# A fused conv, attention and FFN kernel: q, k and v kept in SBUF, twelve units of projections ahead, and a rewritten first seven units

## The chip, the cores and the metric

The kernel runs on one core of one Trainium2 chip. The metric is the device time of one launch in microseconds (us); lower is better. Engines: PE is the matrix engine (PEld its weight loads), DVE the vector engine, ACT the scalar engine, POOL the GpSimd engine, SP the engine whose queue issues most DMAs.

## The reference, cut to what matters

The input x is 64 batches of 64 rows by 1024 values, all in 32-bit floats.

```python
# per batch b, in this order
y   = agg_w[b] @ x + agg_b[b]                      # 64x64 mixing of the rows, from a small MLP on cond
q   = einsum('bsD,Ddh->bsdh', y, Wq) + bq          # 32 x 32 heads;  k, v: 32 values a row
p   = softmax(einsum('bsdh,bse->bsde', q, k) / sqrt(32))   # summed over the heads, so q is 32 values a row
x   = x + broadcast(einsum('bsde,bse->bsd', p, v)) # o: 32 values a row, each repeated 32 times
c   = grouped_conv1d(x, 4 groups, 9 taps) + context(b) + bias
out = x + c @ (scale * (unpacked 4-bit weights - zero_point)).T + bias
```

The softmax works on 32 by 32 values for each of the 4096 rows, and the product with the 1024 by 1024 weights on all rows.

## The kernel before

**Tiling.** A unit is four batches, 256 rows, in two tiles of 128 rows (t = 0, 1). There are 16 units (`NU`) and 32 tiles (`k = 2 * unit + t`). What each unit goes through:

- PE, `project`: z = x times the summed q, v, k weights, 32 matmuls in all (two records for each of 16); ACT copies z from PSUM to SBUF (`z_copy`). PE, `mix`: the mixing over rows, into the PSUM bank `p_sm`.
- DVE, attention: `softmax_top` (adds the bias to q, k, v and finds a bound of each row's scores, a chain of small operations), then for each tile `score` (q times k, 1024 values a partition), `subtract` (the bound), ACT's `exp`, and again on DVE `sum_exp`, `times_v`, `sum_v`, `divide`, which gives o.
- o has to be spread over the channel layout of the convolution. SP's queue writes it to DRAM (`save_o`) and reads it back, repeated, as `o_c` (`spread_o`).
- POOL: `add_o` adds `o_c` to `xc` (three operations for each of four channel groups g), ACT makes the high part `c_hi` (`c_high`), POOL the low part `c_lo` (`c_low`). POOL also makes x + bias (`x_bias`) and adds o there (`x_o`) for the residual.
- PE, `conv`: 6 matmuls of 512 columns for each g. ACT `u_copy`, DVE `turn_u` (a transpose into PSUM), ACT `u_high`, DVE `u_low`. PE, `linear(k, slot)`: 8 slots of 4 matmuls, 512 columns each, for a tile. DVE `finish` adds the result to the residual, SP stores it.

**What sets the order.** Every engine runs a list of calls written out by hand. For the first units it is a written list (SP, POOL, ACT, DVE and PE each have theirs); from unit 5 of the attention on, a loop with a fixed order per unit. An engine starts an instruction when the one before it has left and the semaphores it waits for have come.

**Where operands lie.** In the kernel before, q and v of a unit stay in the PSUM bank `p_sm`, as does the bound `top` from unit 2 on (units 0 and 1 have it in SBUF, `top_own`); only k is copied to SBUF (`k_sb`, L812). The sum `num` is in PSUM as well. So DVE's `score` (L828) reads `p_sm` and `k_sb`, `subtract` (L833) `prob` and `p_sm`, `times_v` (L841) `prob` and `p_sm`, `divide` (L860) `p_sm` and `rden`. POOL's operands are all in SBUF. Only units 1 and 0 have some `subtract` calls on POOL (L476).

**The first unit** is special: its o doesn't go over DRAM. PE copies it with a selection matrix (`copy_o`, L1217) and DVE adds it to `xc` out of PSUM (`add_first`, L868, eight operations). Unit 1's tile edges and two `c_low` calls of position p = 2 are DVE's (L876, L882); both operands of these four instructions are in SBUF.

Of the kernel before, what the change touches and what calls it, by code (L numbers as in the profile page):

```python
# [44 lines left out]

def block_program(nc, xt_in, xc_in, cols, mix_w, wq, wvk, conv_w, ctx_w, packed_t, xn_in, bias_in, out):
    ctx = ExitStack()
    with ctx:
# [1417 lines left out]
```

## Time and profile before

| | |
|---|---|
| time, median of 3 runs | 431.02 us (429.46 to 432.3) |
| the profiled execution's own time | 432.14 us |
| its span, first to last instruction | 430.2 us |
| mean granted PE clock | 0.992 |
| busy in the span: PE, DVE, POOL, ACT | 412.6, 363.5, 340.9, 226.8 us |

Busy time of an engine is the time in which at least one of its instructions is in the engine. Matmul records overlap each other, so a PE that is busy all the time is only at its pace if the number of its matmuls in a stretch says so too. The duration of a DVE or POOL instruction includes any time that it stands in its engine and can't go on, which the views of idle time and waits don't show; it shows where the same shape takes longer in one place than in another.

### The profile page before, as it was taken

The page shows a single profiled execution, that of the slowest core. Times are in us where ns is not written, and L with a number is a line of the kernel's source. Part 1 is how long each engine was busy: PE and PEld are TensorE (multiplying, and loading weights), DVE is VectorE, ACT ScalarE, POOL GpSimd, SP SyncE. Part 2 cuts the span into 40 slices and gives each one's busy share as a digit, 9 for nine tenths or more (in the row PEclk, how much of TensorE's full clock was granted, in tenths as well). Part 3 has the DMA queues.
Part 4 walks back from the last instruction along what each step waited for, and adds up shares of the span by engine and source line. Part 5 has one row for each costly group of instructions (what it writes and reads, how often), then busy time and mean ns, then how long its engine had stood idle before and what let it go on. Part 6 is the DMA issues. An engine that isn't in the chain of part 4 may idle for free.

```text
span 430.2 us, 6661 instructions
## 1 busy us (share of the span) xinstructions
PE 412.6 (96%) x2195; PEld 348.8 (81%) x2195; DVE 363.5 (85%) x603; ACT 226.8 (53%) x465; POOL 340.9 (79%) x316
## 2 busy tenths in 40 slices
PE   3969899899999999999999999999999999999997
PEld 2969799778888888888888888888888888888885
DVE  2896999998989899899989799998989799983421
ACT  3854655556455274657446365647264465562700
POOL 4033948769686999999999979899979979999920
PEclk9988999999999999999999999999999999999999
DMA  8989246470637565664736290928174371816112
GB/s 312 385 330 379 102 149 225 146 270 5 182 106 265 192 220 202 181 240 143 281 100 223 62 350 20 329 88 259 63 237 185 69 254 38 287 41 234 48 52 98
DMA packets 21752, 79.05 MB, mean 184 GB/s; under 512 B 5704, under 2 KB 5832, under 8 KB 17352
## 3 DMA queue, kind: packets, MB, share of 16 engines
q1 hardware_dynamic: 21416, 77.21, 51.2%
q10 hardware_dynamic: 288, 1.18, 0.9%
q8 instruction: 33, 0.54, 0.5%
q14 instruction: 15, 0.12, 0.1%
HBM read 61.11 MB, written 17.27 MB: 182 GB/s over the span
## 4 chain that ended last, share of the span: by engine, by line
PE 79%; DVE 6%; DMA 2%; issue 1%; POOL 1%; ACT 0%; DVEq 0%; POOLq 0%
PE p_f L1159 51%; PE p_conv L1153 19%; PE p_sm L1129 7%; PE p_sm L1138 1%; DMA o_c<-o_dram 1%; DMA o_dram<-o_sb 1%; DVE den L837 1%; DVE c_lo L882 1%; DVE xc L876 1%; DVE prob L828 1%; DVE prob L833 1%; DVE p_sm L845 1%; POOL xc L440 0%; DVE p_ut L893 0%; DVE prob L841 0%
## 5 line engine op out<-in xcount | busy, mean ns | idle before, releaser
L1159 PE MATMUL p_f<-w_ffn,u_hi 128*128 128x512 f32 x512 | 195.8, 392 | 0.0
L1159 PE MATMUL p_f<-w_ffn,u_lo 128*128 128x512 f32 x512 | 194.9, 390 | 0.0
L610 ACT ACTIVATE u_sb<-p_conv,u_bias,cols_sb 128x128 f32<-128x128 f32 x256 | 95.0, 460 | 42.2 <-PE p_conv L1153 40.2
L1159 PEld LDWEIGHTS p_f<-w_ffn,u_lo 128*128 128x128 f32 x512 | 96.2, 188 | 20.5
L1159 PEld LDWEIGHTS p_f<-w_ffn,u_hi 128*128 128x128 f32 x512 | 96.1, 188 | 20.5
L453 POOL TENSOR_TENSOR c_lo<-xc,c_hi 128x516 fp32r<-128x516 f32 (+1 forms) x66 | 82.7, 1263 | 11.6 <-ACT c_hi L600 6.8
L464 POOL TENSOR_TENSOR xn<-xn,bias_n 128x1024 f32<-128x1024 f32 x32 | 76.3, 2403 | 4.7 <-DMA xn<-xn_in_in 4.6
L600 ACT ACTIVATE c_hi<-xc 128x516 fp32r<-128x516 f32 (+1 forms) x68 | 41.0, 608 | 65.0 <-POOL xc L445 59.8
L440 POOL TENSOR_TENSOR xc<-xc,o_c 128x384 f32<-128x384 f32 x60 | 54.3, 905 | 24.5 <-DMA o_c<-o_dram 23.3
L906 DVE TENSOR_TENSOR xn<-p_f,xn 128x512 f32<-128x512 f32 x64 | 43.4, 678 | 23.8 <-PE p_f L1159 23.4
L893 DVE STREAM_TRANSPOSE p_ut<-u_sb 128x512 f32<-128x512 f32 (+1 forms) x68 | 45.8, 680 | 16.4 <-ACT u_sb L610 16.3
L471 POOL TENSOR_TENSOR xn<-xn,o_sb 128x1024 f32<-128x1024 f32 x30 | 57.1, 1922 | 0.2
L1153 PE MATMUL p_conv<-c_hi,cw_hi 128*128 128x512 f32 (+1 forms) x136 | 54.2, 399 | 2.0 <-DVE c_lo L882 1.2
L619 ACT ACTIVATE u_hi<-p_ut 128x512 fp32r<-128x512 f32 (+1 forms) x68 | 39.2, 577 | 31.5 <-DVE p_ut L893 31.1
L1153 PE MATMUL p_conv<-c_lo,cw_hi 128*128 128x512 f32 (+1 forms) x136 | 52.4, 385 | 0.0
L1153 PE MATMUL p_conv<-c_hi,cw_lo 128*128 128x512 f32 (+1 forms) x136 | 52.4, 385 | 0.0
L1129 PEld LDWEIGHTS p_sm<-w,xt 128*128 128x128 f32 x416 | 49.6, 194 | 2.5 <-issue 1.5
L1129 PE MATMUL p_sm<-w,xt 128*128 128x96 f32 x416 | 50.0, 277 | 0.9 <-issue 0.8
L592 ACT ACTIVATE prob<-prob 128x1024 f32<-128x1024 f32 x32 | 33.8, 1055 | 24.9 <-DVE prob L833 21.2
L897 DVE TENSOR_TENSOR u_lo<-p_ut,u_hi 128x512 fp32r<-128x512 f32 (+1 forms) x68 | 42.3, 641 | 0.3 <-ACT u_hi L619 0.3
L837 DVE TENSOR_REDUCE den<-prob 128x32 f32<-128x1024 f32 x32 | 37.9, 1208 | 1.4 <-ACT prob L592 1.3
L845 DVE TENSOR_REDUCE p_sm<-prob 128x32 f32<-128x1024 f32 x32 | 38.9, 1216 | 0.1
(113 smaller groups left out, 458.6 us busy)
## 6 DMA issues: line engine op xcount, KB each, us to landing
xc<-xc_in_in SPq DMA_DIRECT2D x16, 1032.0 KB, 8.8
xn<-xn_in_in SPq DMA_DIRECT2D x16, 1024.0 KB, 7.1
out<-xn SPq DMA_DIRECT2D x31, 512.0 KB, 7.0
xt<-xt_in_in SPq DMA_DIRECT2D x15, 1024.0 KB, 5.6
o_c<-o_dram SPq DMA_DIRECT2D x15, 256.0 KB
xn<-wq_in SPq DMA_DIRECT2D x4, 512.0 KB, 12.4
xt<-wq_in SPq DMA_DIRECT2D x1, 1024.0 KB, 6.8
xn<-wq_in SPq DMA_DIRECT2D x1, 1024.0 KB, 8.8
```

The costliest lines, as they stand in the source:

```text
L440: eng.tensor_tensor(x4[:, :, :, 0:3], x4[:, :, :, 0:3], o.unsqueeze(3).broadcast_to([P, UB, DH, 3]), ALU.add).then_inc(s_add, 1)
L453: eng.tensor_tensor(rows_of(c_lo, p, g), rows_of(xc[:, unit_of(p) % 2, :, :, :], p, g), rows_of(c_hi, p, g).bitcast(F32), ALU.subtract).th ...
L464: eng.tensor_tensor(x, x, bias_n[:, :], ALU.add).then_inc(s_xb, 1)
L471: eng.tensor_tensor(runs, runs, o_val(k).unsqueeze(2).broadcast_to([P, DH, D // DH]), ALU.add).then_inc(s_xo, 1)
L610: ins = eng.activation(u_sb[:, g % 2, i * P:(i + 1) * P], p_conv[g % 2][:, i * P:(i + 1) * P], ACT.Identity, bias=u_bias[:, g, bat:bat + 1 ...
L845: eng.tensor_reduce(num(a)[:, t, :], prob[:, t, :, :], AX.X, ALU.add).then_inc(s_num, 1)
L893: eng.transpose(columns(p_ut[g % 2], p), columns(u_sb[:, g % 2, :], p)).then_inc(s_ut, 1)
L897: eng.tensor_tensor(ut_view(u_lo, p, g), columns(p_ut[g % 2], p).rearrange("p (n r c) -> p n r c", n=len(batches(p)), r=R), ut_view(u_hi, ...
L906: eng.tensor_tensor(x, p_f[half][:, :], x, ALU.add).then_inc(s_res, 1)
L1129: last = mm(z_ps(a)[:, t * W3:(t + 1) * W3], xt[:, a % NXT, r, t * P:(t + 1) * P], w3[:, r, :], start=(r == 0), stop=(r == R - 1))
L1153: last = mm(columns(p_conv[g % 2], p), w[:, shift, g, :], rows_of(src, p, g)[:, :, shift:shift + P], start=(n == 0), stop=(n == 5))
L1159: return mm(p_f[half][:, :], u[:, (k // TU) % 2, r, t * P:(t + 1) * P], w_ffn[:, r, 512 * half:512 * half + 512], **flags)
```

## The change

1. **q, k, v, the bound and num in SBUF.** `softmax_top` adds the bias in one operation from PSUM into a new SBUF tile `qkv_sb` (two buffers). `score`, `subtract`, `times_v` and `divide` now read `qkv_sb`, `top_own` and `num`, all in SBUF. The column sums that the bias needs are kept in SBUF too (`col_sb`). One PSUM bank then serves the mixing of all units, and `mix(a)` waits only until unit a - 1's bias is added.
2. **z up to 12 units ahead** (`NZ` 7 to 12), with three x buffers in place of two; units 0 to 10 are projected in the written part.
3. **o of unit 0 over DRAM too** (`spread_first`, one transfer for each tile); `copy_o` and `add_first` are gone, and POOL's `add_o` does positions 0 and 1 as well (8 groups of three half-size operations).
4. **A new beginning**: q weights in nine transfers, sums over heads interleaved with the small MLP, the context weights with the other small inputs, zero-point work on POOL, and warming matmuls before the first real ones.
5. **New written lists** for the first seven units on all engines; the loops start later, with the same order inside.
6. **The last half tile in quarters**: the second half of tile 31 in two pieces of 256 columns, each added and stored by itself.

```diff
-        k_sb = sb("k_sb", [P, TU, DH])
+        num = sb("num", [P, TU, DH])
+        qkv_sb = sb("qkv_sb", [P, 2, TU, W3])
+        col_sb = sb("col_sb", [P, W3])
...
         def qkv(a):
-            return p_sm[a % 2][:, 0:TU * W3].rearrange("p (t w) -> p t w", t=TU)
+            return qkv_sb[:, a % 2, :, :]
...
         def top(a):
-            return p_sm[a % 2][:, TU * W3:TU * W3 + TU * DH].rearrange("p (t d) -> p t d", t=TU)
...
+            return top_own[:, a % 2, :, :]
...
                 for t in range(TU):
-                    eng.scalar_tensor_tensor(out=qkv_bias[:, t, :], in0=col3(a if a else 1), scalar=mix_bias[:, TU * a + t:TU * a + t + 1],
+                    eng.scalar_tensor_tensor(out=qkv_bias[:, t, :], in0=col_sb[:, :], scalar=mix_bias[:, TU * a + t:TU * a + t + 1],
                                              in1=bias3[:, :], op0=ALU.mult, op1=ALU.add).then_inc(s_qb, 1)
...
-                eng.tensor_tensor(k_sb[:, :, :], qkv(a)[:, :, 2 * DH:W3], qkv_bias[:, :, 2 * DH:W3], ALU.add).then_inc(s_qkv, 1)
-                eng.tensor_tensor(qkv(a)[:, :, 0:2 * DH], qkv(a)[:, :, 0:2 * DH], qkv_bias[:, :, 0:2 * DH], ALU.add).then_inc(s_qkv, 1)
+                eng.tensor_tensor(qkv(a), mixed_ps(), qkv_bias[:, :, :], ALU.add).then_inc(s_qkv, 1)
...
-                eng.tensor_tensor(prob[:, t, :, :], down(qkv(a)[:, t, 0:DH]), along(k_sb[:, t, :]), ALU.mult).then_inc(s_score, 1)
+                eng.tensor_tensor(prob[:, t, :, :], down(qkv(a)[:, t, 0:DH]), along(qkv(a)[:, t, 2 * DH:W3]), ALU.mult).then_inc(s_score, 1)
...
-                eng.tensor_reduce(num(a)[:, t, :], prob[:, t, :, :], AX.X, ALU.add).then_inc(s_num, 1)
+                eng.tensor_reduce(num[:, t, :], prob[:, t, :, :], AX.X, ALU.add).then_inc(s_num, 1)
...
-                eng.tensor_tensor(o_val(k), num(a)[:, t, :], rden[:, t, :], ALU.mult).then_inc(s_o, 1)
+                eng.tensor_tensor(o_val(k), num[:, t, :], rden[:, t, :], ALU.mult).then_inc(s_o, 1)
...
-NZ = 7
+NZ = 12
+LAST = ((0, 512), (512, 768), (768, 1024))
...
+            def spread_first(t):
+                eng.wait_ge(s_ow, 16 * (t + 1))
+                eng.dma_start(o_c[:, 0, t * TN:(t + 1) * TN, :, :].rearrange("p n g d -> p (n g d)"),
+                              o_dram[0, :, t * TN * G:(t + 1) * TN * G, :].rearrange("c k d -> c (k d)").unsqueeze(0).broadcast_to([R, CG, TN * G * DH])).then_inc(s_oc_first[t], 16)
```

**DVE in the loop, the second tile's scores to the first o.** The names are those of the list above; `xn<-p_f,xn` is `finish`. Before:

```order
L828 TENSOR_TENSOR prob<-p_sm,k_sb 128x1024
L833 TENSOR_TENSOR prob<-prob,p_sm 128x1024
L906 TENSOR_TENSOR xn<-p_f,xn 128x512
L837 TENSOR_REDUCE den<-prob 128x32 x2
L841 TENSOR_TENSOR prob<-prob,p_sm 128x1024 x2
L845 TENSOR_REDUCE p_sm<-prob 128x32
L906 TENSOR_TENSOR xn<-p_f,xn 128x512
L849 RECIPROCAL rden<-den 128x32
L860 TENSOR_TENSOR o_sb<-p_sm,rden 128x32
```

The same place in the changed kernel:

```order
L960 TENSOR_TENSOR prob<-qkv_sb 128x1024
L965 TENSOR_TENSOR prob<-prob,top_own 128x1024
L1024 TENSOR_TENSOR xn<-p_f,xn 128x512
L969 TENSOR_REDUCE den<-prob 128x32 x2
L973 TENSOR_TENSOR prob<-prob,qkv_sb 128x1024 x2
L977 TENSOR_REDUCE num<-prob 128x32
L1024 TENSOR_TENSOR xn<-p_f,xn 128x512
L981 RECIPROCAL rden<-den 128x32
L987 TENSOR_TENSOR o_sb<-num,rden 128x32
```

The order is the same. In the four kinds of `TENSOR_TENSOR` other than `finish`, the operand that was in PSUM (`p_sm`) is now in SBUF (`qkv_sb`, which `score` reads twice, `top_own`, `num`).

**DVE in the loop, `softmax_top`.** Before:

```order
L802 SCALAR_TENSOR_TENSOR qkv_bias<-p_sm,mix_bias,bias 128x96 x2
L812 TENSOR_TENSOR k_sb<-p_sm,qkv_bias 128x64
L813 TENSOR_TENSOR p_sm<-p_sm,qkv_bias 128x2x64
L817 TENSOR_REDUCE k_max<-k_sb 128x2
L817 TENSOR_REDUCE k_min<-k_sb 128x2
L821 TENSOR_TENSOR p_sm<-p_sm,k_max 128x64
L821 TENSOR_TENSOR top<-p_sm,k_min 128x64
L823 TENSOR_TENSOR p_sm<-p_sm,top 128x64
```

In the changed kernel:

```order
L937 SCALAR_TENSOR_TENSOR qkv_bias<-col_sb,mix_bias,bias 128x96 x2
L945 TENSOR_TENSOR qkv_sb<-p_sm,qkv_bias 128x192
L949 TENSOR_REDUCE k_max<-qkv_sb 128x2
L949 TENSOR_REDUCE k_min<-qkv_sb 128x2
L952 TENSOR_TENSOR top_own<-qkv_sb,k_max 128x64
L952 TENSOR_TENSOR top<-qkv_sb,k_min 128x64
L954 TENSOR_TENSOR top_own<-top_own,top 128x64
```

One operation fewer, and five of the seven two-operand ones now have both tensors in SBUF.

**DVE at the start, from the bound of unit 1 to o of unit 0's second tile.** Before:

```order
L823 TENSOR_TENSOR top_own<-p_sm,top 128x64
L868 TENSOR_TENSOR xc<-p_f,xc 128x2x129
L837 TENSOR_REDUCE den<-prob 128x32
L828 TENSOR_TENSOR prob<-p_sm,k_sb 128x1024
L841 TENSOR_TENSOR prob<-prob,p_sm 128x1024
L868 TENSOR_TENSOR xc<-p_ut,xc 128x2x129
L845 TENSOR_REDUCE p_sm<-prob 128x32
L868 TENSOR_TENSOR xc<-p_ut,xc 128x2x129
L868 TENSOR_TENSOR xc<-p_f,xc 128x2x129
L849 RECIPROCAL rden<-den 128x32
L854 TENSOR_TENSOR o_first<-p_sm,rden 128x128
```

In the changed kernel:

```order
L954 TENSOR_TENSOR top_own<-top_own,top 128x64
L977 TENSOR_REDUCE num<-prob 128x32
L981 RECIPROCAL rden<-den 128x32
L987 TENSOR_TENSOR o_sb<-num,rden 128x32
L969 TENSOR_REDUCE den<-prob 128x32
L960 TENSOR_TENSOR prob<-qkv_sb 128x1024
L973 TENSOR_TENSOR prob<-prob,qkv_sb 128x1024
L977 TENSOR_REDUCE num<-prob 128x32
L981 RECIPROCAL rden<-den 128x32
L987 TENSOR_TENSOR o_sb<-num,rden 128x32
```

`add_first` (L868) is gone from DVE, and the bound of unit 1 comes before the last steps of unit 0's first tile.

## Rows read from the trace of the kernel before

**Rows 1.** The page, part 1: busy us (share of the span) and number of instructions.
```profile
PE 412.6 (96%) x2195; PEld 348.8 (81%) x2195; DVE 363.5 (85%) x603; ACT 226.8 (53%) x465; POOL 340.9 (79%) x316
```

**Rows 2.** Windows: stretch, its length, busy us (instructions), granted clock, DMA share, GB/s.
```profile
0.00:40.00 40.00, 29.49 (x246) 27.69 (x247) 25.40 (x54) 24.04 (x30) 9.83 (x12) 0.91 0.90 356
106.18:380.22 274.04, 274.04 (x1345) 229.41 (x1344) 255.00 (x418) 148.75 (x314) 249.68 (x239) 1.00 0.53 180
```

**Rows 3.** Timeline of DVE and POOL, 66 to 79 us: start, duration, engine, instruction.
```profile
66.04 0.90 POOL L440 TENSOR_TENSOR xc<-xc,o_c 128x384 f32<-128x384 f32 x1 [7.03 <-DMA o_c<-o_dram]
66.15 1.74 DVE L876 TENSOR_TENSOR xc<-xc,o_c 64x512 f32<-64x512 f32 x1
67.01 1.51 POOL L440 TENSOR_TENSOR xc<-xc,o_c 128x384 f32<-128x384 f32 x1
67.92 1.53 DVE L876 TENSOR_TENSOR xc<-xc,o_c 64x512 f32<-64x512 f32 x1
...
70.62 0.69 DVE L882 TENSOR_TENSOR c_lo<-xc,c_hi 128x516 fp32r<-128x516 f32 x1
...
72.14 4.74 POOL L464 TENSOR_TENSOR xn<-xn,bias_n 128x1024 f32<-128x1024 f32 x2
...
74.62 2.82 DVE L882 TENSOR_TENSOR c_lo<-xc,c_hi 128x516 fp32r<-128x516 f32 x1
...
76.82 1.76 POOL L453 TENSOR_TENSOR c_lo<-xc,c_hi 128x516 fp32r<-128x516 f32 x1
```

**Rows 4.** DVE's groups by shape: instruction, count, busy us, mean ns, idle before.
```profile
L828 DVE TENSOR_TENSOR prob<-p_sm,k_sb 128x1024 f32<-128x1024 f32 x32 | 38.6, 1207 | 0.0
L841 DVE TENSOR_TENSOR prob<-prob,p_sm 128x1024 f32<-128x1024 f32 x32 | 37.7, 1210 | 0.0
L833 DVE TENSOR_TENSOR prob<-prob,p_sm 128x1024 f32<-128x1024 f32 x28 | 33.8, 1209 | 0.4
L802 DVE SCALAR_TENSOR_TENSOR qkv_bias<-p_sm,mix_bias,bias 128x96 f32<-128x96 f32 x32 | 8.6, 309 | 6.9 <-PE p_sm L1138 6.0 <-PE p_sm L1252 0.9
L860 DVE TENSOR_TENSOR o_sb<-p_sm,rden 128x32 f32<-128x32 f32 x30 | 5.8, 192 | 2.8
L868 DVE TENSOR_TENSOR xc<-p_f,xc 128x258 f32<-128x258 f32 x4 | 1.7, 415 | 1.0 <-PE p_ut L1217 1.0
L833 DVE TENSOR_TENSOR prob<-prob,top_own 128x1024 f32<-128x1024 f32 x1 | 1.2, 1224 | 0.0
```

**Rows 5.** POOL's groups by shape, with the same columns.
```profile
L464 POOL TENSOR_TENSOR xn<-xn,bias_n 128x1024 f32<-128x1024 f32 x32 | 76.3, 2403 | 4.7 <-DMA xn<-xn_in_in 4.6
L453 POOL TENSOR_TENSOR c_lo<-xc,c_hi 128x516 fp32r<-128x516 f32 x58 | 76.2, 1323 | 4.8 <-POOL xc L445 2.0
L471 POOL TENSOR_TENSOR xn<-xn,o_sb 128x1024 f32<-128x1024 f32 x30 | 57.1, 1922 | 0.2
L440 POOL TENSOR_TENSOR xc<-xc,o_c 128x384 f32<-128x384 f32 x60 | 54.3, 905 | 24.5 <-DMA o_c<-o_dram 23.3
L443 POOL TENSOR_TENSOR xc<-xc,o_c 64x128 f32<-64x128 f32 x56 | 29.4, 525 | 0.0
```

**Rows 6.** Timeline of DVE at the start: the wait for unit 1's mixing, unit 1's last o.
```profile
36.30 0.54 DVE L802 SCALAR_TENSOR_TENSOR qkv_bias<-p_sm,mix_bias,bias 128x96 f32<-128x96 f32 x2 [2.97 <-PE p_sm L1138]
...
57.54 0.19 DVE L860 TENSOR_TENSOR o_sb<-p_sm,rden 128x32 f32<-128x32 f32 x1
```

**Rows 7.** Timeline at the end: the last o, POOL's add and last c_lo, DVE's last u_lo.
```profile
381.88 0.19 DVE L860 TENSOR_TENSOR o_sb<-p_sm,rden 128x32 f32<-128x32 f32 x1
...
389.49 0.89 POOL L440 TENSOR_TENSOR xc<-xc,o_c 128x384 f32<-128x384 f32 x1
...
401.44 1.31 POOL L453 TENSOR_TENSOR c_lo<-xc,c_hi 128x516 fp32r<-128x516 f32 x1
...
409.68 0.68 DVE L897 TENSOR_TENSOR u_lo<-p_ut,u_hi 128x512 fp32r<-128x512 f32 x1
```

**Rows 8.** The chain that ended last, from 406 us on: start us, us, what.
```profile
406.05 20.91 PE p_f L1159 x92
426.95 0.02 issue
426.98 0.69 DVE xn L906
```

More of the change, by code:

```diff
@@ L380, in _ @@
             spread_o(3)
+            store(0)
             load_c(4)
@@ L1006, in _ @@
             u_low(2, 1)
-            score(3, 1)
-            turn_u(2, 3)
             finish(1, 0)
             u_low(2, 2)
+            subtract(3, 1)
+            turn_u(2, 3)
+            sum_exp(3, 0)
             u_low(2, 3)
-            subtract(3, 1)
+            times_v(3, 0)
+            sum_exp(3, 1)
+            sum_v(3, 0)
             finish(1, 1)
-            sum_exp(3, 0)
-            turn_u(3, 0)
-            sum_exp(3, 1)
-            times_v(3, 0)
-            finish(2, 0)
             times_v(3, 1)
-            u_low(3, 0)
@@ L1033, in _ @@
             turn_u(3, 3)
+            sum_exp(4, 0)
             u_low(3, 2)
[L1035 removed]
             u_low(3, 3)
[L1037 removed]
+            sum_exp(4, 1)
+            times_v(4, 0)
             finish(3, 1)
[L1039 to L1046 removed]
+            times_v(4, 1)
+            sum_v(4, 0)
+            divide(4, 0)
@@ L1047, in _ @@
+            sum_v(4, 1)
+            divide(4, 1)
+            finish(4, 0)
             turn_u(4, 0)
-            divide(4, 1)
-            finish(4, 1)
             softmax_top(5)
-            turn_u(4, 1)
             u_low(4, 0)
             score(5, 0)
+            turn_u(4, 1)
+            finish(4, 1)
+            score(5, 1)
+            subtract(5, 0)
             u_low(4, 1)
-            subtract(5, 0)
             turn_u(4, 2)
+            turn_u(4, 3)
+            subtract(5, 1)
+            u_low(4, 2)
@@ L1057, in _ @@
             finish(5, 0)
-            turn_u(4, 3)
-            u_low(4, 2)
             u_low(4, 3)
-            for i in range(5, NU + 2):
+            sum_exp(5, 0)
+            finish(5, 1)
+            sum_exp(5, 1)
+            times_v(5, 0)
+            turn_u(5, 0)
+            times_v(5, 1)
+            sum_v(5, 0)
+            divide(5, 0)
+            u_low(5, 0)
+            sum_v(5, 1)
+            divide(5, 1)
+            finish(6, 0)
+            softmax_top(6)
+            turn_u(5, 1)
@@ new lines, in _ @@
+            turn_u(5, 2)
+            score(6, 0)
+            finish(6, 1)
+            subtract(6, 0)
+            u_low(5, 1)
+            score(6, 1)
+            turn_u(5, 3)
+            sum_exp(6, 0)
+            u_low(5, 2)
+            u_low(5, 3)
+            finish(7, 0)
+            subtract(6, 1)
+            times_v(6, 0)
+            finish(7, 1)
+            sum_exp(6, 1)
+            sum_v(6, 0)
+            turn_u(6, 0)
+            times_v(6, 1)
+            finish(8, 0)
+            softmax_top(7)
@@ L1063, in _ @@
+            turn_u(6, 1)
+            divide(6, 0)
+            sum_v(6, 1)
+            divide(6, 1)
+            u_low(6, 0)
+            score(7, 0)
+            u_low(6, 1)
+            finish(8, 1)
+            turn_u(6, 2)
+            subtract(7, 0)
+            turn_u(6, 3)
+            u_low(6, 2)
+            finish(9, 0)
+            u_low(6, 3)
+            for i in range(7, NU + 2):
                 a, b, d = i, i - 1, i - 2
```

979 lines of the change are left out of this document (579 added, 400 removed).

## The prediction

> **What bounds the kernel now.** I read the page's busy times first, then windows, then DVE's and POOL's timelines side by side. PE is busy for 412.6 of 430.2 us, DVE for 363.5, POOL for 340.9 [rows 1]. The first 40 us are the beginning: PE is busy for 29.5 of them at a granted clock of 0.91, and POOL for only 9.8 [rows 2]. In the long middle, 106.18 to 380.22 us, twelve units go by, 274.04 / 12 = 22.84 us each. PE has no idle time there and 1.00 of its clock. DVE is busy for 255.0 us, 21.25 a unit, and POOL for 249.7, 20.8 a unit [rows 2]. So PE sets the period, but DVE has only 1.6 us a unit to spare and POOL 2.0. A change that lengthens either by more than that takes the bound from PE.
>
> The row that decides is in the timeline of these two engines. Four DVE instructions of the old kernel read two tensors in SBUF while POOL is at work, and they run very unevenly. L882 takes 0.69 us at 70.62 and 2.82 us at 74.62, same shape [rows 3]. The second began just after POOL had begun an `x_bias` (the pair runs from 72.14 to 76.88) and ended 0.56 us after that one's end. POOL's next, `c_low`, then took 1.76 us where 1.32 is its mean [rows 3, 5]. The two L876 and two L440 take turns: POOL 0.90, DVE 1.74, POOL 1.51 where 0.905 is usual, DVE 1.53 [rows 3, 5]. DVE's last ends after POOL's has ended at 68.52. So each stands until the other's instruction is over, and a waiting instruction goes in before the other engine's next one.
>
> In contrast, DVE's wide operations with one input in PSUM mean 1207, 1209 and 1210 ns over 92 instructions, though POOL is at work beside most of them [rows 4]: no collision.
>
> **Part 1, q, k, v, bound and num in SBUF.** This is the term that counts. It turns these DVE instructions of every unit into ones with two SBUF inputs: `score` x2, `subtract` x2, `times_v` x2 (six of 1.21 us, 7.26 us) and seven small ones, two of the bias (0.31) and three of the bound and two of `divide` (0.19 to 0.23), 1.6 us together [rows 4]. Sum 8.9 us, about 8.7 as they stand in the engine with their overlaps. Their own duration doesn't change: with `top_own` in SBUF and POOL idle beside it, `subtract` took 1224 ns against 1209 [rows 4]. What they do to each other:
>
> - POOL. It reads SBUF in every instruction of a unit and must stand still for DVE's 8.7 us: 20.8 + 8.7 = 29.5 us a unit at least.
> - DVE. A unit's POOL work is twenty instructions: two of 2.40, four of 1.31, two of 1.92, four of 0.905, eight of 0.525 (L443 and its twin) [rows 5], sum 21.7 us, mean 1.09. A DVE instruction that meets one finds on average sum(L^2) / (2 sum(L)) = 0.72 us of it left. One that follows another such DVE instruction finds a whole one, 1.09, since POOL's waiting one goes in between. The thirteen stand in eight groups in DVE's order (`score` with `subtract`; the two `times_v`; two single `divide`s; the two of the bias; the three of the bound; `score`; `subtract`). So 8 x 0.72 + 5 x 1.09 = 11.2 us, times the share of time in which POOL has work, 29.5 / 31.5 = 0.94: 10.5 us. One small instruction less saves 0.2. DVE's unit becomes 21.25 - 0.2 + 10.5 = 31.5 us.
>
> DVE's 31.5 is the later of the two, and PE's 22.8 is far below. I take 31.5 a unit. The low end is 28.1: only the six wide ones collide and POOL bounds (20.8 + 7.3). The high end is 34: every one of the thirteen waits for a whole POOL instruction (13 x 1.0 on 21.05).
>
> The Trainium skill, "SBUF — State Buffer", section "Who interferes with whom", says that a DVE instruction with two SBUF inputs contends with a GpSimd one that reads SBUF, and that whichever starts first holds the shared ports for its whole length. The rows above agree for L876 and L882. What no run here has yet shown is an operand repeated by a zero stride, as q, k, v and the bound are; by the page these collide as well, which gives the 31.5 and not PE's 22.8.
>
> **Part 2, z twelve units ahead, and `mix` free of the old waits.** PE's projections move from the middle to the beginning. That would shorten PE's units, but PE is no longer the bound: worth nothing in the middle.
>
> **Parts 3 to 5, the beginning.** DVE loses eight L868 of 0.41 us, 3.3 us, the idle 2.97 us before unit 1's bias and the 1.0 before the first L868 [rows 4, 6], and about 1.8 us of zero-point operations: 9 us off the way to unit 1's last o, which is at 57.7 us now [rows 6]. Against that, POOL now works earlier (8 groups of `add_o` at half size, some 9 us) and DVE's instructions with two SBUF inputs meet it: about 7 us, most of one unit's 10.5 at POOL's lower share. Net -2: unit 1 ends at 55.7. Bounds 48 and 63. The o of unit 0 over DRAM comes about 7.4 us later than from PE, like the last one, 382.07 to 389.49 [rows 7]; the projections up to unit 8 stand in PE's list in that time and hide it.
>
> **Part 6, the last half tile in quarters.** 32 matmuls of 256 columns for 16 of 512, then a shorter add and store at the end. Less than 1 us either way, taken as 0.
>
> **The end.** From unit 15's last o: 382.07 to 410.36, 28.3 us over DRAM, POOL, ACT, PE and DVE to the last `u_low` [rows 7]. PE will have no backlog by then, so the last two tiles' 64 matmuls follow at 20.91 / 92 = 0.227 us each, 14.5 us [rows 8], then add and store as now, 430.2 - 426.98 = 3.2. Together 46.0 us; it is 48.1 now.
>
> **The sum.** 55.7 + 14 units x 31.5 + 46.0 = 542.7 us of span. The profiled execution's own time is 1.9 above its span and 1.1 above the median of its runs, so I forecast 543.5, rounded 543 us.
>
> **The rivals.**
>
> A: the operands that a zero stride repeats don't collide, or not enough to matter, and PE stays the bound. For it: the four colliding instructions in the trace read no DVE operand that way, and the `subtract` that does had an idle POOL. Against: POOL's L440 reads `o_c` repeated three times, and it did stand still. Then the beginning counts: of the 9 us saved on DVE, PE keeps about 5, for it can't start before the weights have come, and is filled with projections instead of idling in between; 431 - 5 = 426, at best 418. This ends on the other side. It decides if DVE's added waits stay below the 1.6 us a unit that DVE has to spare. 9 in 100, with 3 in 100 more for a small collision that cancels the gain, 428 to 435.
>
> B: only the wide operations collide, or DVE's small ones slip in between POOL's instructions; POOL bounds at 28.1. 55.7 + 14 x 28.1 + 46 = 495. With a collision that is only part of each instruction, 26 a unit, 466. For it: L882 needed 0.56 us after POOL's end, less than its 0.69, so part of it had run already. 28 in 100.
>
> C: PE, now idle for some 28% of each unit, loses its clock. In the first 40 us, where it was busy for 29.5, the clock was 0.91. PE's 22.8 us stretched to 31.5 still fits if less than 38% of its work runs at the lower level of 1.2 GHz; beyond that it costs. If 60% does, a unit is 36.5 and the time 613. The Trainium skill, "TensorE: Matmul & The Clock Gate", section "HAM oscillation — how this bites in real kernels", warns of just such gaps; a trace with long stretches below 1.00 would bear it out. 7 in 100.
>
> My forecast's own case, 29 to 34 a unit, has 53 in 100, 508 to 578.
>
> **The numbers.** Below 480 lie A, the small collision and a fifth of B, 17 in 100; above 582 about 4. So the range is 480 to 582. A measurement of this kernel can tell about 1% from no change. Faster by over 1%: 0.09. Within 1%: 0.03. Slower by over 1%: 0.88.
>
> **What would show it.** Right: DVE's 1024-wide `score`, `subtract` and `times_v` mean about 1.9 to 2.2 us in place of 1.21, while `sum_exp` and `sum_v` (one input) stay at 1.21; POOL's `c_low` means over 1.6; PE idle for a quarter of the middle, waiting for `c_lo` or `u_lo`; a period of 31.5 us. Wrong: those three at 1.21 beside a busy POOL (A), or POOL busy all the time and DVE with gaps (B), or the clock below 0.9 in the middle (C). If the small ones stay at 0.2 to 0.3 us while the wide ones grow, B's price holds.

## The result, and the profile after

The changed kernel takes 538.41 us (median of 4 runs, 536.82 to 539.82) against 430.78 us for the kernel before (4 runs): a ratio of 1.2483, 95% interval 1.2447 to 1.2519. That is 4.6 us under the forecast of 543 and 107.6 us slower than before. The profiled execution took 536.82 us, with a span of 535.0.

The page's first part, after (busy us, share of the span, instructions), and the waits of the whole span (us in total, times, longest):

```profile
PE 451.0 (84%) x2149; PEld 368.7 (69%) x2149; DVE 474.3 (89%) x575; ACT 219.8 (41%) x464; POOL 423.5 (79%) x348
```

```profile
ACT u_hi L719 <- DVE p_ut L1010: 119.2, 40, 8.8
ACT c_hi L700 <- POOL xc L509: 91.0, 39, 5.8
PE p_f L1339 <- DVE xn L1024: 39.9, 14, 5.7
...
PE p_conv L1333 <- POOL c_lo L516: 28.4, 16, 4.0
```

DVE has 28 instructions fewer than before and is busy for 110.8 us longer; POOL for 82.6 us longer [rows 1]. PE, which had no idle time in the middle [rows 2], now waits, most of all for DVE's `finish` and POOL's `c_low`. The same stretch of twelve units as before, from the first o of unit 3 to the first of unit 15 (length, busy us of PE, PEld, DVE, ACT, POOL, granted clock, DMA share, GB/s):

```profile
118.57:484.74 366.17, 305.56 (x1270) 241.67 (x1269) 356.21 (x410) 147.64 (x314) 307.98 (x240) 0.91 0.38 130
```

A unit takes 366.17 / 12 = 30.5 us, where it was 22.84. DVE is busy for 29.7 of them, 97%; POOL for 25.7, PE for 25.5. So DVE sets the period. Its groups by shape (count, busy us, mean ns, idle before), to be held against [rows 4]:

```profile
L973 DVE TENSOR_TENSOR prob<-prob,qkv_sb 128x1024 f32<-128x1024 f32 x32 | 54.7, 1730 | 0.0
L937 DVE SCALAR_TENSOR_TENSOR qkv_bias<-col_sb,mix_bias,bias 128x96 f32<-128x96 f32 x32 | 48.8, 1562 | 0.0
L965 DVE TENSOR_TENSOR prob<-prob,top_own 128x1024 f32<-128x1024 f32 x29 | 47.1, 1624 | 0.3
L960 DVE TENSOR_TENSOR prob<-qkv_sb 128x1024 f32<-128x1024 f32 x32 | 43.1, 1349 | 0.0
...
L977 DVE TENSOR_REDUCE num<-prob 128x32 f32<-128x1024 f32 x32 | 38.6, 1206 | 0.0
...
L987 DVE TENSOR_TENSOR o_sb<-num,rden 128x32 f32<-128x32 f32 x32 | 29.6, 924 | 6.9 <-POOL xn L534 4.2
L952 DVE TENSOR_TENSOR top_own<-qkv_sb,k_max 128x64 f32<-128x64 f32 x16 | 13.8, 861 | 0.0
```

`sum_v` (L977, one input) is at 1.21 us. Everything with two SBUF inputs has grown, and the small ones by the largest factor: the bias from 309 to 1562 ns, `divide` from 192 to 924. POOL's groups, against [rows 5]:

```profile
L516 POOL TENSOR_TENSOR c_lo<-xc,c_hi 128x516 fp32r<-128x516 f32 x58 | 80.7, 1400 | 26.0 <-issue 19.5 <-ACT c_hi L700 3.0 <-POOL xc L509 1.0
L527 POOL TENSOR_TENSOR xn<-xn,bias_n 128x1024 f32<-128x1024 f32 x32 | 79.2, 2490 | 0.1
L504 POOL TENSOR_TENSOR xc<-xc,o_c 128x384 f32<-128x384 f32 x60 | 77.7, 1296 | 30.8 <-DMA o_c<-o_dram 29.5
```

And the collision itself, the timeline of DVE and POOL in the same microseconds (start, duration, engine, instruction):

```profile
242.88 2.42 DVE L952 TENSOR_TENSOR top<-qkv_sb,k_min 128x64 f32<-128x64 f32 x1
245.34 2.31 DVE L954 TENSOR_TENSOR top_own<-top_own,top 128x64 f32<-128x64 f32 x1
```

```profile
242.84 4.73 POOL L527 TENSOR_TENSOR xn<-xn,bias_n 128x1024 f32<-128x1024 f32 x2
247.53 3.79 POOL L534 TENSOR_TENSOR xn<-xn,o_sb 128x1024 f32<-128x1024 f32 x2
```

Two DVE operations of 0.23 us each take 2.42 and 2.31 us, because each stands until one of the two `x_bias` instructions of POOL is over. The `x_bias` pair itself, 4.73 us, is no longer than in the kernel before (4.74 in [rows 3]).

### The profile page after: what moved, and what is told of

It is laid out like the page before. It is cut to its first block and busy times, and to the rows that moved or that the text cites. A ratio compares the mean times of both kernels' runs of the same rounds, so it can differ in the third digit from the quotient of the medians.

```text
span 535.0 us, 6609 instructions
## 1 busy us (share of the span) xinstructions
PE 451.0 (84%) x2149; PEld 368.7 (69%) x2149; DVE 474.3 (89%) x575; ACT 219.8 (41%) x464; POOL 423.5 (79%) x348
## 5 line engine op out<-in xcount | busy, mean ns | idle before, releaser
L1339 PE MATMUL p_f<-w_ffn,u_hi 128*128 128x512 f32 (+1 forms) x512 | 214.7, 426 | 43.3 <-DVE xn L1024 39.9
L1339 PE MATMUL p_f<-w_ffn,u_lo 128*128 128x512 f32 (+1 forms) x512 | 210.2, 421 | 0.0
L1339 PEld LDWEIGHTS p_f<-w_ffn,u_hi 128*128 128x128 f32 x512 | 105.8, 207 | 75.7 <-DVE xn L1024 38.8
L1339 PEld LDWEIGHTS p_f<-w_ffn,u_lo 128*128 128x128 f32 x512 | 105.7, 208 | 23.8 <-issue 0.6
L504 POOL TENSOR_TENSOR xc<-xc,o_c 128x384 f32<-128x384 f32 (+1 forms) x68 | 81.9, 1206 | 33.9 <-DMA o_c<-o_dram 32.5
L710 ACT ACTIVATE u_sb<-p_conv,u_bias,cols_sb 128x128 f32<-128x128 f32 x256 | 94.4, 466 | 25.8 <-PE p_conv L1333 25.5
L534 POOL TENSOR_TENSOR xn<-xn,o_sb 128x1024 f32<-128x1024 f32 x32 | 64.8, 2041 | 0.1
L973 DVE TENSOR_TENSOR prob<-prob,qkv_sb 128x1024 f32<-128x1024 f32 x32 | 54.7, 1730 | 0.0
L1333 PEld LDWEIGHTS p_conv<-c_hi,cw_hi 128*128 128x128 f32 x136 | 26.2, 193 | 40.7 <-issue 31.5
L507 POOL TENSOR_TENSOR xc<-xc,o_c 64x128 f32<-64x128 f32 (+1 forms) x64 | 51.5, 805 | 0.0
L937 DVE SCALAR_TENSOR_TENSOR qkv_bias<-col_sb,mix_bias,bias 128x96 f32<-128x96 f32 x32 | 48.8, 1562 | 0.0
L509 POOL TENSOR_TENSOR xc<-xc,o_c 64x128 f32<-64x128 f32 (+1 forms) x64 | 43.9, 686 | 4.8
```

The lines of the kernel that those rows point to most:

```text
L504: eng.tensor_tensor(x4[:, :, :, 0:3], x4[:, :, :, 0:3], o.unsqueeze(3).broadcast_to([P, n, DH, 3]), ALU.add).then_inc(s_add, 1)
L507: eng.tensor_tensor(x4[0:64, :, :, 3], x4[0:64, :, :, 3], o[0:64], ALU.add).then_inc(s_add, 1)
L509: eng.tensor_tensor(x0[64:P, :, :, 0], x0[64:P, :, :, 0], o[64:P], ALU.add).then_inc(s_add, 1)
L534: eng.tensor_tensor(runs, runs, o_val(k).unsqueeze(2).broadcast_to([P, DH, D // DH]), ALU.add).then_inc(s_xo, 1)
L710: ins = eng.activation(u_sb[:, g % 2, i * P:(i + 1) * P], p_conv[g % 2][:, i * P:(i + 1) * P], ACT.Identity, bias=u_bias[:, g, bat:bat + 1 ...
L937: eng.scalar_tensor_tensor(out=qkv_bias[:, t, :], in0=col_sb[:, :], scalar=mix_bias[:, TU * a + t:TU * a + t + 1], in1=bias3[:, :], op0=AL ...
```

## The experiments

The theory that the runs test is the prediction's: a whole-instruction lock between DVE instructions with two SBUF inputs and POOL instructions that read SBUF, so part 1 alone costs the 107 us. Each engine stands until the other's instruction is over. Rivals: the new order and beginning cost it (parts 2 to 5), SBUF inputs are slower by themselves, or PE's clock costs it.

### Part 1 alone, in the kernel before

```diff
-        k_sb = sb("k_sb", [P, TU, DH])
+        num_sb = sb("num_sb", [P, TU, DH])
+        qkv_sb = sb("qkv_sb", [P, 2, TU, W3])
+        col_sb = sb("col_sb", [P, W3])
...
-                eng.tensor_tensor(prob[:, t, :, :], down(qkv(a)[:, t, 0:DH]), along(k_sb[:, t, :]), ALU.mult).then_inc(s_score, 1)
+                eng.tensor_tensor(prob[:, t, :, :], down(qkv_sb[:, a % 2, t, 0:DH]), along(qkv_sb[:, a % 2, t, 2 * DH:W3]), ALU.mult).then_inc(s_score, 1)
```

> The kernel before, with part 1 of the change alone: q, k, v, bound, num and column sums in SBUF, all queues' orders as before. Collision theory (a DVE instruction with two SBUF inputs and a POOL instruction stand for each other): DVE's unit grows from 22.8 to about 30.4 us as in the changed kernel, 57.7 + 6 + 14 x 30.4 + 48 = 537, range 520 to 550. Rival 'order' (the new lists for the first units and the z's twelve ahead put DVE late): no more than 435 here. Rival 'operand' (SBUF inputs are slower by themselves): score, subtract, times_v longer even where POOL is idle; 500 to 540 too, but then with one even duration.

Measured: 536.75 us (532.9 to 538.73), ratio 1.2416 (1.2359 to 1.2473). Its twelve units in the middle:

```profile
120.45:486.63 366.18, 307.46 (x1343) 246.69 (x1342) 359.04 (x406) 145.02 (x309) 305.77 (x238) 0.91 0.38 134
```

366.18 us, where the changed kernel has 366.17. With the old order, the old beginning and seven units of z, part 1 gives 105.5 of the 107.6 us. The rival of the order falls. The expectation of 537 us rested on the changed kernel's own 30.4 us a unit, so its being met shows that the unit is the same, and nothing on the size of the waits. The edit also carries a build option of the changed kernel, `dynamic_dma_scratch_size=2048`; the kernel with the operands back in PSUM, below, has it too and takes 435.89 us, so it isn't what costs the time.

### Operands back in PSUM: a control, and all of them

The changed kernel needs both small banks for mixing and z, so a bank that DVE has to itself must be made first. The control does only that: mixing and the late z share `p_sm[1]`, the z of units before 9 use the `p_f` banks, and `mix(3)` follows z of unit 10 in PE's list, for which ACT copies that z earlier. All operands stay in SBUF.

```diff
-            return p_sm[0][:, 0:TU * W3].rearrange("p (t w) -> p t w", t=TU)
+            return p_sm[1][:, 2 * W3:2 * W3 + TU * W3].rearrange("p (t w) -> p t w", t=TU)
...
-            return (p_f[1] if a in Z_EARLY else p_sm[1])[:, 0:TU * W3]
+            return (p_f[a % 2] if a < 9 else p_sm[1])[:, 0:TU * W3]
```

> The changed kernel with other PSUM banks, all operands of the attention still in SBUF: mixing in bank p_sm[1], early z in p_f[0] and p_f[1], mix(3) after z of unit 10. It is the control for the next kernel. All theories: 538 within 6 us, since PE is not the bound.

Measured: 542.87 us (540.45 to 544.87), ratio 1.2585 (1.2531 to 1.264). Against the changed kernel's own ratio of 1.2483 the banks themselves cost 0.8%, 4.5 us. That comes before the middle: the twelve units take 365.29 us, no longer than the changed kernel's, but start 6.8 us later (125.41 against 118.57).

The second kernel is the control with q, v, the bound, `num` and the column sums in `p_sm[0]`; k stays in SBUF. So the addition that fills q, k and v is split in two, as in the kernel before: DVE has one small instruction more a unit.

```diff
-                eng.tensor_tensor(prob[:, t, :, :], down(qkv(a)[:, t, 0:DH]), along(qkv(a)[:, t, 2 * DH:W3]), ALU.mult).then_inc(s_score, 1)
+                eng.tensor_tensor(prob[:, t, :, :], down(qv_ps(a)[:, t, 0:DH]), along(qkv(a)[:, t, 2 * DH:W3]), ALU.mult).then_inc(s_score, 1)
```

> As the control, but q, v, bound, num and column sums in PSUM bank p_sm[0], which DVE alone uses after the start; k in SBUF. Collision theory: the wide operations are back at 1.21 us, PE bounds again at 22.8 a unit less the z's that are done early, 415 to 428. Rival 'order': 530 or more, as the control. Rival 'operand': 415 to 428 as well.

Measured: 435.89 us (434.73 to 437.58), ratio 1.0098 (1.0067 to 1.0129). Two of its DVE groups, and its twelve units:

```profile
L968 DVE TENSOR_TENSOR prob<-p_sm,qkv_sb 128x1024 f32<-128x1024 f32 x32 | 38.6, 1209 | 0.0
L981 DVE TENSOR_TENSOR prob<-prob,p_sm 128x1024 f32<-128x1024 f32 x32 | 38.0, 1209 | 0.0
```

```profile
106.91:385.93 279.02, 273.06 (x1269) 224.20 (x1269) 256.85 (x421) 149.27 (x315) 252.87 (x241) 0.99 0.50 171
```

107.0 of the control's 542.9 us go when the operands move; `score` and `times_v` are back at 1209 ns and the clock at 0.99. So the clock was a result, not a cause. But I had expected 415 to 428 us, and 435.9 is above that: in this bank arrangement the rest of the change brings no gain, but 4.7 us of loss. Unit 1 is done at 54.30, 3.4 us earlier than before, but PE, which idles for 3.9 us of 60 between 40 and 100 us before, idles here for 5.7, and for 6.0 of the twelve middle units, where it had none:

```profile
PE p_conv L1343 <- POOL c_lo L522: 5.9, 4, 3.0
PE p_f L1349 <- ACT low L689: 3.2, 1, 3.2
```

The waits of PE between 54 and 180 us are mostly for `c_lo`, which needs the o of the attention, and once for a z copy. The clock adds to it: 0.94 from 40 to 100 us, where it was 1.00 before. Whether the new lists or the shared banks cause the 4.7 us was not tried.

### Which operands carry it

The control, with only `num` and the column sums in PSUM. Nine of a unit's thirteen instructions keep two SBUF inputs: the six wide ones and three small ones of the bound.

```diff
-        num = sb("num", [P, TU, DH])
...
-        col_sb = sb("col_sb", [P, W3])
...
+        col_sb = p_sm[0][:, 384:480]
+        num = p_sm[0][:, 320:384].rearrange("p (t d) -> p t d", t=TU)
```

> The control with other PSUM banks, but with num and the column sums in PSUM: of a unit's thirteen DVE instructions with two SBUF inputs, four small ones (two of the bias, two divides) get a PSUM input; the three of the bound and the six wide ones stay. In the changed kernel those four took 40.1 + 23.4 = 63.5 us more than before, 4.0 a unit. Theory of the lock, by those rows: DVE's unit falls from 30.4 to 26.4, but POOL still stands still for the other 7.9 us of DVE's, 28.7 a unit, so POOL bounds: 542.9 - 15 x 1.7 = 517, with 500 to 525 as its range; DVE's bias and divide at 0.31 and 0.19 us. Rival, the wide ones carry the loss: within 5 us of the control, 538 to 548. Rival, each removed wait is handed to the next instruction with two SBUF inputs: as the wide ones carry it, but with score, subtract and times_v longer by 0.3 to 0.7 us than in the control.

The control, with q, v and the bound in PSUM, `num` and the column sums in SBUF: four small instructions a unit keep two SBUF inputs.

```diff
+        def qv_ps(a):
+            return p_sm[0][:, a % 2 * 128:a % 2 * 128 + 2 * TU * DH].rearrange("p (t w) -> p t w", t=TU)
+
+        def top_ps():
+            return p_sm[0][:, 256:320].rearrange("p (t d) -> p t d", t=TU)
```

> The control with other PSUM banks, but with q, v and the bound in PSUM and num and the column sums in SBUF: only the four small instructions (two of the bias, two divides, 1.0 us a unit) keep two SBUF inputs. Theory of the lock: POOL stands still for 1.0 us a unit only, 21.8; DVE pays a POOL instruction's rest for each of the four, 4.0 a unit as in the changed kernel, 21.05 + 4.0 = 25.1 a unit, against 23.8 with all in PSUM: 436 + 15 x 1.3 = 455, with 440 to 465 as its range; bias and divide still over 0.9 us each. Rival, what counts is how long DVE holds the ports (1.0 of 8.9 us): a ninth of the loss of 107 us, 436 + 12 = 448, with bias and divide near 0.5 us. Rival, a small instruction waits as long as a wide one and four of thirteen cost four thirteenths: 436 + 33 = 469.

Measured: 516.34 us (513.25 to 517.64), ratio 1.194 (1.1873 to 1.2007) for the first, 477.13 us (474.83 to 478.58), ratio 1.1055 (1.0998 to 1.1111) for the second. Groups of the first kernel, and its twelve units:

```profile
L952 DVE TENSOR_TENSOR top<-qkv_sb,k_min 128x64 f32<-128x64 f32 x16 | 24.9, 1554 | 0.0
L954 DVE TENSOR_TENSOR top_own<-top_own,top 128x64 f32<-128x64 f32 x16 | 19.1, 1194 | 0.5
L952 DVE TENSOR_TENSOR top_own<-qkv_sb,k_max 128x64 f32<-128x64 f32 x16 | 17.8, 1110 | 0.0
```

```profile
122.32:464.21 341.89, 292.83 (x1270) 231.44 (x1269) 331.29 (x410) 147.00 (x313) 314.07 (x240) 0.95 0.41 139
```

And of the second, two groups over all of its span, then its twelve units:

```profile
L943 DVE SCALAR_TENSOR_TENSOR qkv_bias<-col_sb,mix_bias,bias 128x96 f32<-128x96 f32 x32 | 46.3, 1487 | 5.5 <-PE p_sm L1328 5.5
...
L995 DVE TENSOR_TENSOR o_sb<-num,rden 128x32 f32<-128x32 f32 x32 | 25.9, 810 | 5.5 <-POOL xn L540 1.9 <-DVE rden L989 0.5 <-issue 0.4
```

```profile
109.14:423.62 314.48, 280.41 (x1271) 224.39 (x1270) 308.49 (x422) 148.52 (x316) 253.75 (x241) 0.98 0.44 151
```

The first lands on the theory's 517, but not by the theory's way, so the match is luck. I had DVE at 26.4 us a unit and POOL as the bound, at 28.7. Measured, a unit takes 28.5 us, DVE is busy for 27.6 of them (97%) and POOL for 26.2: DVE still sets the period, and two errors met. One is that POOL stands still for less than all of DVE's time. The other is that waits come back elsewhere. In the control the three operations of the bound took 30.4 us in all; here they take 61.8. The bias and the divides got 64 us shorter, and half of that came back in the bound, whose operations are the next that can collide after the bias. So the rival of handed-on waits is half right too, only that the small ones take them, not the wide ones, whose means moved by 0.16 us at most.

The second shows what four tiny instructions cost. Their own work is 1.0 us a unit, and the kernel is 41.2 us slower than with all in PSUM. In the middle a unit takes 26.2 us against 23.25, DVE is 98% busy, and POOL's 253.75 us are as good as unchanged from 252.87. I had expected 455, with 440 to 465, and 469 for the rival that counts instructions; both are too low. The four small ones' added time was 3.6 us a unit over the run (37.7 us for the bias and 19.8 for the divides, over 16 units), near the expected 4.0. In the middle it is more: DVE is busy for 4.3 us a unit longer than with all in PSUM. And I had taken a unit with all in PSUM at 23.8 us, where it is 23.25. The rival by held time (448) falls clearly: what a small DVE instruction costs is what POOL has under way when it comes, not its own length.

### POOL's long instructions in pieces

The changed kernel with `x_bias` and `x_o` each cut in four pieces of 256 columns.

```diff
-                x = xn[:, u % NXN, k % TU, :]
-                eng.tensor_tensor(x, x, bias_n[:, :], ALU.add).then_inc(s_xb, 1)
+                for c in range(4):
+                    x = xn[:, u % NXN, k % TU, 256 * c:256 * c + 256]
+                    ins = eng.tensor_tensor(x, x, bias_n[:, 256 * c:256 * c + 256], ALU.add)
+                ins.then_inc(s_xb, 1)
```

> The changed kernel with POOL's x_bias and x_o (1024 columns, 2.4 and 1.9 us) in four instructions of 256 columns each, about 0.6 us. Collision theory with a lock for a whole instruction: DVE's small operations that now wait out an x_bias (bias of qkv 1.56 us mean for 0.31 of work) wait for a quarter of it, below 0.9 mean; DVE's waits fall from 7.4 to about 4.5 us a unit; 538 - 14 x 3 = 496, range 485 to 520, though POOL has 12 instructions a unit more. Rival 'operand', or a lock that is shared in proportion instead of held: no gain, 538 or more, for POOL does more.

Measured: 528.43 us (526.28 to 529.56), ratio 1.2268 (1.2236 to 1.23). One DVE group, the two of POOL, and the twelve units:

```profile
L942 DVE SCALAR_TENSOR_TENSOR qkv_bias<-col_sb,mix_bias,bias 128x96 f32<-128x96 f32 x32 | 21.6, 712 | 0.0
```

```profile
L528 POOL TENSOR_TENSOR xn<-xn,bias_n 128x256 f32<-128x256 f32 x128 | 106.2, 864 | 0.1
L538 POOL TENSOR_TENSOR xn<-xn,o_sb 128x256 f32<-128x256 f32 x128 | 103.8, 845 | 0.1
```

```profile
119.41:469.77 350.36, 293.61 (x1251) 233.25 (x1250) 313.99 (x409) 147.23 (x311) 337.34 (x377) 0.93 0.39 136
```

DVE's bias fell from 1562 to 712 ns, as a lock that lasts for one instruction of POOL says, and the divides from 924 to 409. But I had 496 us for it and got 10 us in all. The reason is in the other two views: four pieces take 4 x 0.86 = 3.5 us where one instruction took 2.5, 66 us more in all for the two kinds, and POOL is now busy for 28.1 of 29.2 us a unit. The bound went from DVE to POOL. The mechanism held, the sum left out what pieces cost POOL. How much of that is the pieces' own cost and how much is time that each piece stands still for DVE was not separated; in the kernel below, four pieces beside small DVE instructions take 4 x 0.72 = 2.9 us, where the whole one takes 2.34.

### The rule by itself

A kernel with DVE and POOL alone, in stages set apart by semaphores; it computes nothing of the reference. "two", "small" and "quarter" have two SBUF inputs, of 1024, 64 and 256 columns. The list of stages, its lines joined:

```python
STAGES = (            # POOL's operation, how many, DVE's operation, how many
    (None, 0, "two", 4), (None, 0, "repeated", 4), (None, 0, "small", 8), ("two", 4, None, 0),
    ("two", 8, "two", 8), ("two", 8, "repeated", 8), ("two", 8, "small", 16), ("two", 8, "psum", 8),
    ("two", 8, "reduce", 8), ("memset", 8, "two", 8), ("one", 8, "two", 8),
    ("quarter", 16, "small", 16), ("two", 8, "wide_small", 16))
```

> Nothing of the reference is computed: DVE and POOL only, in thirteen stages set apart by semaphores. First each alone, then POOL's 128x1024 add with two SBUF inputs, eight times, beside each of DVE's kinds: two plain SBUF inputs, two inputs repeated by a zero stride, 128x64 with two SBUF inputs, one input in PSUM, a reduction; then DVE's plain two inputs beside POOL's memset (writes only) and beside POOL with one input; then DVE's 128x64 beside POOL's 128x256; last DVE's reduction and 128x64 in turn. Theory of the lock (each stands until the other's instruction is over, and they take turns): two beside two 3.6 us each on both engines (1.2 + 2.4), the repeated inputs the same, 128x64 about 2.5, PSUM input and reduction 1.2 as alone and POOL 2.4 as alone; 128x64 beside 128x256 about 0.7; beside POOL with one input about 3.6 or less by POOL's own time. Rival, the ports are shared while both run: 2.4 on DVE for the wide ones and 0.2 to 0.3 for 128x64. Beside the memset: 1.2 if only POOL's reads count, over 2 if its writes do.

Groups by stage, each fence one stretch. A stage's first DVE instruction starts before POOL's and is free, and some at a stage's end run alone, so DVE's means beside POOL are a little low. Each alone:

```profile
L99 DVE TENSOR_TENSOR v_out<-v_a,v_b 128x1024 f32<-128x1024 f32 x4 | 4.6, 1220 | 0.1
L101 DVE TENSOR_TENSOR v_out<-v_a,v_b 128x1024 f32<-128x1024 f32 x4 | 4.6, 1220 | 0.1
L107 DVE TENSOR_TENSOR v_out<-v_a,v_b 128x64 f32<-128x64 f32 x8 | 1.2, 220 | 0.1
```

```profile
L75 POOL TENSOR_TENSOR g_out<-g_a,g_b 128x1024 f32<-128x1024 f32 x4 | 9.2, 2339 | 19.6 <-DVE v_out L107 19.6
```

Two plain inputs beside POOL's add, then (L101) two inputs repeated by a zero stride beside the same:

```profile
L75 POOL TENSOR_TENSOR g_out<-g_a,g_b 128x1024 f32<-128x1024 f32 x8 | 26.3, 3325 | 0.2 <-POOL g_out L75 0.2
L99 DVE TENSOR_TENSOR v_out<-v_a,v_b 128x1024 f32<-128x1024 f32 x8 | 24.2, 3090 | 9.5 <-POOL g_out L75 9.5
```

```profile
L75 POOL TENSOR_TENSOR g_out<-g_a,g_b 128x1024 f32<-128x1024 f32 x8 | 26.3, 3324 | 0.2 <-POOL g_out L75 0.2
L101 DVE TENSOR_TENSOR v_out<-v_a,v_b 128x1024 f32<-128x1024 f32 x8 | 24.2, 3089 | 2.3 <-POOL g_out L75 2.3
```

128x64 beside POOL's add (the last two of the ten run when POOL is done), then one input in PSUM beside the same:

```profile
L107 DVE TENSOR_TENSOR v_out<-v_a,v_b 128x64 f32<-128x64 f32 x10 | 18.7, 1942 | 2.3 <-POOL g_out L75 2.3
L75 POOL TENSOR_TENSOR g_out<-g_a,g_b 128x1024 f32<-128x1024 f32 x8 | 18.5, 2340 | 0.2 <-POOL g_out L75 0.2
```

```profile
L75 POOL TENSOR_TENSOR g_out<-g_a,g_b 128x1024 f32<-128x1024 f32 x8 | 18.5, 2348 | 1.2 <-DVE v_out L107 1.2
L103 DVE TENSOR_TENSOR v_out<-v_a,v_ps 128x1024 f32<-128x1024 f32 x8 | 9.1, 1215 | 0.1
```

Beside POOL's memset, and beside POOL with one SBUF input:

```profile
L99 DVE TENSOR_TENSOR v_out<-v_a,v_b 128x1024 f32<-128x1024 f32 x8 | 9.2, 1219 | 9.5 <-POOL g_out L75 9.5
L77 POOL MEMSET g_out<- 128x1024 f32 x8 | 7.2, 952 | 0.1
```

```profile
L79 POOL TENSOR_SCALAR g_out<-g_a 128x1024 f32<-128x1024 f32 x4 | 13.1, 3299 | 2.1 <-DVE v_out L99 2.1
L99 DVE TENSOR_TENSOR v_out<-v_a,v_b 128x1024 f32<-128x1024 f32 x8 | 12.5, 1634 | 0.1
```

128x64 beside POOL's add of 256 columns:

```profile
L81 POOL TENSOR_TENSOR g_out<-g_a,g_b 128x256 f32<-128x256 f32 x16 | 11.0, 719 | 0.2 <-POOL g_out L79 0.2
L107 DVE TENSOR_TENSOR v_out<-v_a,v_b 128x64 f32<-128x64 f32 x16 | 10.4, 724 | 11.7 <-POOL g_out L79 11.7
```

The lock holds between two adds, and both engines pay for wide against wide: 3.36 us for each of DVE's after the free first one (8 x 3.09 less 1.22, over 7) and 3.32 for POOL's, nearly the sum of 1.22 and 2.34. Inputs repeated by a zero stride collide like others, which no run had shown until now. The rival that SBUF inputs are slower by themselves falls: alone they take 1220 ns. One input in PSUM: 1215 ns, no collision; a reduction, which has one input: 1210. The small one costs DVE nearly a whole POOL instruction, 19.4 us for ten with 0.22 us of work each, and POOL nothing (2340 ns against 2339 alone). When reductions of 1.2 us and small ones take turns beside POOL's add, a small one takes 1.26 us: it pays the rest of POOL's instruction, not a whole one. The sharing rival, 2.4 and 0.3 us, falls. Against POOL with one SBUF input the lock isn't whole: 1634 ns in the mean, where standing for a whole instruction of 2.77 us would give some 4 us.

### Part 6 alone, in the kernel before

```diff
+LAST = ((0, 512), (512, 768), (768, 1024))
...
-                x = xn[:, (k // TU) % NXN, k % TU, 512 * half:512 * half + 512]
-                eng.tensor_tensor(x, p_f[half][:, :], x, ALU.add).then_inc(s_res, 1)
+                at, end = parts(k)[half]
+                x = xn[:, (k // TU) % NXN, k % TU, at:end]
+                eng.tensor_tensor(x, ffn_ps(k, half), x, ALU.add).then_inc(s_res, 1)
```

> The kernel before with part 6 alone, the last half tile in quarters. The prediction's term was less than 1 us either way. The last add is 256 wide in place of 512 (0.69 us, so some 0.3 less), the last store half as large; 16 matmuls more, each of half the columns. Gain of 0.3 to 0.9 us: 430.3. Rival: the added matmuls' fixed cost outweighs it, 431.2 to 432.

Measured: 430.78 us (430.02 to 431.39, 12 runs) against 431.68, ratio 0.9971 (0.9951 to 0.9991). Its last adds:

```profile
424.53 0.42 DVE L915 TENSOR_TENSOR xn<-p_f,xn 128x256 f32<-128x256 f32 x1 [1.11 <-PE p_f L1169]
426.33 0.42 DVE L915 TENSOR_TENSOR xn<-p_conv,xn 128x256 f32<-128x256 f32 x1 [1.38 <-PE p_conv L1169]
```

The last add takes 0.42 us in place of 0.69. The gain of 0.9 us (by the interval, 0.4 to 2.1) is small but real. Of the versions run it is the only one that is faster than the kernel before.

## Why the prediction was right, and where it was off

The forecast was the sum 55.7 + 14 x 31.5 + 46.0 = 542.7. Measured, by the ends of the same instructions:

```profile
61.12 0.25 DVE L987 TENSOR_TENSOR o_sb<-num,rden 128x32 f32<-128x32 f32 x1
```

```profile
486.55 2.15 DVE L987 TENSOR_TENSOR o_sb<-num,rden 128x32 f32<-128x32 f32 x1
```

61.4 + 14 x 30.52 + 46.3 = 535.0, with (488.70 - 61.37) / 14 = 30.52 and 535.0 - 488.7 = 46.3. The span is 7.7 us under the sum. The fourteen units came out 13.7 us shorter, the beginning 5.7 longer, so two errors partly cancel. The median lies only 4.6 us under the forecast, because it is 1.6 above the profiled execution, where I had taken it to be 1.1 below. Within that, the nearness is luck; the range doesn't need it.

- **The mechanism: right, and shown.** Part 1 alone gives 536.75 us, and moving the operands back gives 435.89. The Trainium skill, "SBUF — State Buffer", section "Who interferes with whom", names the rule for such pairs, and that it doesn't hold against a POOL instruction that only writes; the stage with the memset agrees (1219 ns against 1220 alone). The Trainium skill, on the same page, section "Summary: rules for kernel authors", also has the one that issues second blocked until the first is over. For two adds the 3.36 and 3.32 us of the wide pair and the 1942 ns of the small one agree; for DVE's add beside POOL with one SBUF input the 1634 ns don't, and there the measurement decides.
- **The signs: some failed, and the waits were put in the wrong places.** `score`, `subtract` and `times_v` were to mean 1.9 to 2.2 us and came at 1.35, 1.62 and 1.73; `c_low` was to be over 1.6 and came at 1.40; PE was to idle for a quarter of the middle and idles for 17%, and it waits more for `finish` than for `c_lo`. `sum_v` at 1.21 us held, and the period came near, 30.5 for 31.5.
- **DVE's added waits: 8.6 us a unit in the middle, predicted 10.5.** DVE is busy for 29.7 us, its own work is 21.05. With 0.8 us of idle time that makes 30.5. The term was mis-sized in its parts too: I let every instruction meet POOL alike. Over the run the small ones carry 84 us more than before (40.1 for the bias, 23.4 for `divide`, 20.9 for the bound) and the wide ones 33. How much each pays hangs on what POOL has in hand at its place in the order. The timeline at 242 us has the bound beside the two `x_bias`, and unit 15's last divide took 2.15 us beside another `x_bias`; `score` grew by only 0.14 us in the mean. I had written that small ones that stay small would hold rival B's price; they did the opposite.
- **POOL: predicted to stand still for 8.7 us a unit, so 29.5 busy; it is 25.7,** 4.9 more than before. The isolated stages show a reason: a small DVE instruction takes nothing from POOL, only wide against wide costs both. And not every wide one met POOL at work. POOL is busy for 84% of the middle and doesn't bound it, so the low end of 28.1, at which POOL was to bound, was taken for the wrong reason.
- **The beginning: 61.4, predicted 55.7,** in its bounds of 48 to 63. With the operands in PSUM unit 1 ends at 54.3, with the control's banks alone at 61.6. So the collisions cost 7.3 there, predicted 7; what was wrong is the 9 us saved on DVE, of which 3.4 arrived. A part is plain in the trace with the operands in PSUM: the new lists put unit 2's bias, bound and first score, some 3.3 us of work, before unit 1's last o (six bias operations by then where there were four, five scores where there were four), which the prediction didn't count. And DVE is idle there for 12.9 us up to that o, 14.9 before, so only 2 of the 4 us of waits went.
- **The end: 46.3, predicted 46.0.** After the last o no DVE instruction with two SBUF inputs is left, so nothing collides. The parts are off and cancel: 27.3 us to the last `u_low`, predicted 28.3; 16.5 from there to the last add, predicted 14.5, though it took 426.98 - 410.36 = 16.6 in the kernel before too [rows 7, 8]; 2.6 for add and store, predicted 3.2. Part 6, taken as 0, is worth 0.9 us in the kernel before.
- **Rival A** had 426 us if nothing collided. Without the collisions of part 1 the change stands at 435.89, though with the control's banks; with its own banks it can't be run that way, so the 426 isn't settled.
- **Rival C** came half: the clock fell to 0.91 in the middle and PE's unit grew from 22.8 to 25.5 us, with 5 us of idle time left in each. The sign for it, a clock below 0.9 in the middle, didn't come. The Trainium skill, "TensorE: Matmul & The Clock Gate", section "HAM oscillation — how this bites in real kernels", warns of such gaps; the trace agrees in that the clock fell (0.91, and 0.99 with the operands in PSUM, where PE idles for 2% of the middle), but the cost was hidden behind DVE.

## What to carry to other kernels

Before an operand of a DVE instruction moves from PSUM to SBUF, count whether the instruction then has two SBUF inputs and what POOL has in hand at that place: each such instruction, however small, may wait for one whole instruction of POOL. Here a PSUM bank for such operands was worth 107 us, and rearranging the banks for it cost 4.5. Cutting POOL's instructions shortens the waits, but pieces cost POOL more than it may have to give. And a wait that is removed should not be booked as gained in full: part of it can come back in the next instruction that can collide.

## What the runs showed of the hardware that was not expected

- The cost of a small locked instruction is one-sided: DVE's 128x64 pays 1.7 us in the mean beside POOL's add, POOL pays nothing (2339 and 2340 ns).
- POOL with a single SBUF input collides only in part: DVE's add had a mean of 1634 ns (2.05 and 1.21 in turn), POOL's 3.1 us against 2765 ns once DVE was done. Its memset doesn't collide (1219 ns against 1220 alone).
- Removed waits are partly handed to the next instruction that can collide: of 64 us taken from the bias and the divides, 31 came back in the bound's operations of 0.23 us of work.
